# Second layer: one mask instruction for two rows on GpSimd, and the right operand packed on VectorE

## The chip, the cores and the metric

The kernel runs on one core of one Trainium2 chip. The metric is the device time of one launch in microseconds. The engines are TensorE (PE in the profile, PEld for its weight loads), VectorE (DVE), ScalarE (ACT), GpSimd (POOL) and SyncE (SP), which here only starts DMAs.

## The reference

The input `x` is a grid of 256 x 256 tokens with 64 channels. Four layers follow each other, each `x = x + layer(group_norm(x))`. The second one, on which everything here turns, is, cut to what matters:

```python
xn = layernorm(x, norm_w, norm_b)
m = mask[..., None]
left  = jnp.einsum('bijd,hd->bijh', xn, w_left)  * m
right = jnp.einsum('bijd,hd->bijh', xn, w_right) * m
left  = (left  * sigmoid(xn @ w_lgate.T)).astype(jnp.bfloat16)
right = (right * sigmoid(xn @ w_rgate.T)).astype(jnp.bfloat16)
out = jnp.einsum('bikh,bjkh->bijh', left, right).astype(jnp.float32)
out = layernorm(out, onorm_w, onorm_b) * sigmoid(xn @ w_ogate.T)
return jnp.einsum('bijh,dh->bijd', out, w_out)
```

`left` and `right` are two 256 x 256 matrices for each of the 64 channels, and the product over `k` is one matrix product for each channel. The first layer is the same in float32; the third and fourth have no mask.

## The kernel before

Each layer runs in three stages, one behind the other, with all engines joining between them.

**The projection** (`project`, for layers 1, 2 and 4) goes over the tokens in 128 steps of half the grid's rows: a step is 512 columns, two rows of the grid for each half, 64 steps in all. A step is written in parts with leads over each other, and every engine runs its own list in a fixed order:

- TensorE: `spread` (L615), `center` (L593, 16 steps ahead), `variance` (L604, 15 ahead), `heads` for both rows (L628), `out_gate` (L635 to L637). `heads` of a row waits until VectorE has read the last step's product of that row out of its bank (`pair_read`).
- ScalarE: the two passes of `square` (L672, L674, 16 steps ahead), a sigmoid for each row (L691), every eighth step `root` with its two table loads, and the output gate (L705).
- VectorE: `norm` two steps ahead (L755, L756), every eighth step the split of the inverse roots into bf16 terms (`split_high`, L731 and L733, and a step later, `split_low`, L739 and L741), then for each row the product of gate and projection (L774), which raises `pair_read`.
- GpSimd: `low_part` two steps ahead (L835), then the mask. In the second layer that is `mask_rows` (L812): it waits for both rows' products, multiplies the left half of both rows in one instruction (L824) and the right half in one for each row (L828). Each L828 raises `lr_done` by one, and the sigmoid two steps on waits for it, since it writes the slot that the mask reads.

The masked rows go into a stage of 16 rows, in one of two buffers, in bf16. Which order the elements have there differs: the left block has 16 channels, each with a run of 16 rows, `(h i)`; the right block has 16 rows, each with a run of 16 channels, `(i h)`. From the stage SP stores the blocks of all 16-channel groups but the first to DRAM, and the first group to its place in SBUF.

**The triangle product** (`triangle`, L988) takes the 64 channels in four groups of 16. The first group is in SBUF already; SP loads the others (L1031), two buffers in turn. For each channel TensorE makes four matmuls of 256 columns (L1070). Their moving operand is the left block in runs of 16 rows. Their stationary operand is, in the second layer, the right block read in place with a stride of 16 channels (`right_of`); in the other layers VectorE first copies it into consecutive columns (`pack`, L1094), into a ring of four or two. In the second layer ScalarE rounds each result to bf16 into a ring of four (L1144), and the rounded matrix is then written into `O`, where a token's channels are neighbours, by GpSimd for even channels (L1132) and by VectorE for odd ones (`spread_out`, L1106). VectorE does nothing else in this stage of this layer.

**The output** (`output`) normalizes, gates, multiplies and adds the residual. The change does not touch it.

Of the kernel before, what the change touches and what calls it, by code (L numbers as in the profile page):

```python
# [28 lines left out]
ALU = mybir.AluOpType  # L29
# [4 lines left out]
P = 128  # L34
S = 256
# [4 lines left out]
ROWS = CH // S  # L40
# [404 lines left out]
def project(nc, n, kind, low, HG, x, a, left_right, blocks, c, k, ps):  # L445
# [11 lines left out]
    with ExitStack() as ctx:  # L457
        def sb(name, shape, dt=F32):
            return ctx.enter_context(nc.sbuf_tensor(f"{name}_{n}", shape, dt))

        xs, zs, sq = sb("xs", [P, 8, CH]), sb("zs", [P, 16, CH]), sb("sq", [P, 2, CH])
        log_var, r, r_rest = sb("log_var", [P, P]), sb("r", [P, P]), sb("r_rest", [P, P])
# [3 lines left out]
        sig, gates = sb("sig", [P, 4, CH]), sb("gates", [P, 4, CH])  # L466
        paired = low == BF16
        stage0 = sb("stage0", [P, 2, 2, 2, C // HG, SEG * HG], low)
        stage = [stage0[:], last_stage(blocks, low, C // HG)]
# [325 lines left out]
        @block.gpsimd  # L795
        def _(pool):
            def mask_pair(i, q, row):
                m = i * BODY + q
                b = q // SCH
                if q % SCH == 0 and row == 0:  # L800

                    pool.wait_ge(c[f"lr_out{b}"].sem, c[f"lr_out{b}"](i * 16 * SEG_PARTS))
                    pool.wait_ge(c[f"first_out{b}"].sem, c[f"first_out{b}"](i * 64))
                pool.wait_ge(c["pair_read"].sem, c["pair_read"](m * 2 + row + 1))
                product = sig[:, (2 * q + row) % 4, :].rearrange("p (a e) -> p a e", a=4)

                by_g = k["mask"][:].rearrange("p g b i -> p (g b) i")
                mk = by_g[:, :, bass.ds(m * ROWS + row, 1)].to_broadcast([P, 4, P])
                pool.tensor_tensor(staged(b, q, row), product, mk,
                                   ALU.mult).then_inc(c["lr_done"].sem, 1)  # L810

            def mask_rows(i, q):  # L812
                m = i * BODY + q
                b = q // SCH
                if q % SCH == 0:
                    pool.wait_ge(c[f"lr_out{b}"].sem, c[f"lr_out{b}"](i * 16 * SEG_PARTS))
                    pool.wait_ge(c[f"first_out{b}"].sem, c[f"first_out{b}"](i * 64))
                pool.wait_ge(c["pair_read"].sem, c["pair_read"](m * 2 + 2))
                slot, at = 2 * q % 4, q % SCH * ROWS
                product = sig[:, slot:slot + 2, :].rearrange("p r (c l n h) -> p l c n h r", c=4, l=2, h=HG)  # L820
                by_g = k["mask"][:].rearrange("p g b i -> p (g b) i")
                mk = by_g[:, :, bass.ds(m * ROWS, ROWS)].unsqueeze(2)
                left = stage[b][:, :, :, 0].rearrange("p g b n (h i) -> p (g b) (n h) i", h=HG)[:, :, :, at:at + ROWS]
                pool.tensor_tensor(left, product[:, 0].rearrange("p c n h r -> p c (n h) r"),  # L824
                                   mk.to_broadcast([P, 4, P // 2, ROWS]), ALU.mult)
                for row in range(ROWS):
                    right = stage[b][:, :, :, 1].rearrange("p g b n (i h) -> p (g b) n i h", h=HG)[:, :, :, at + row]
                    pool.tensor_tensor(right, product[:, 1, :, :, :, row],  # L828
                                       mk[:, :, :, row:row + 1].to_broadcast([P, 4, P // 2 // HG, HG]), ALU.mult).then_inc(c["lr_done"].sem, 1)

            def low_part(i, q):
                m = i * BODY + q
                pool.wait_ge(c["xn_done"].sem, c["xn_done"](m + 1))
                pool.wait_ge(c["hi_done"].sem, c["hi_done"](m + 1))
                pool.tensor_tensor(lo[:, q % 4, :], xn[:, q % 2, :], hi[:, q % 4, :], ALU.subtract).then_inc(c["lo_done"].sem, 1)  # L835

            def step(i, q, more):
                if more(NORM):
                    low_part(i, q + NORM)
                if paired:  # L840
                    mask_rows(i, q)
                elif masked:
                    for row in range(ROWS):
                        mask_pair(i, q, row)

            for q in range(NORM):
                low_part(0, q)
            bodies_of(pool, step)
# [139 lines left out]
def triangle(nc, n, turned, low, H, HG, left_right, blocks, O, c, k, ps):  # L988
# [6 lines left out]
    rounded_first = low == BF16  # L995
    RING = 2 if turned else 4
    with ExitStack() as ctx:  # L997
        left, right = blocks[:, 0], blocks[:, 1]
        stays = turns == 1
        packed = None if rounded_first else ctx.enter_context(nc.sbuf_tensor(f"packed{n}", [P, RING, 2, S], low))  # L1000
        rounded = ctx.enter_context(nc.sbuf_tensor(f"rounded{n}", [P, 4, 2 * S], BF16)) if rounded_first else None
        right_t = ctx.enter_context(nc.sbuf_tensor(f"right_t{n}", [P, 2, 2, S], F32)) if turned else None
        block = ctx.enter_context(nc.Block())

        def channel(t, s, h):
            return t * (2 * HG) + (s * HG + h)

        def right_of(s, h):
            return right[:, s].rearrange("p b s (i h) -> p b (s i) h", h=HG)[:, :, :, h]

        def rows_of(block, s, h):

# [8 lines left out]
        def loaded(t, s):  # L1021

            return c[f"lr_in{s}"](t * 32 + 32 * s)
# [19 lines left out]
        @block.tensor  # L1043
        def _(pe):
            def turn(t, s, h):

                ch = channel(t, s, h)
                pe.wait_ge(c["packed"].sem, c["packed"](ch + 1))
                pe.wait_ge(c["tr_copied"].sem, c["tr_copied"](ch - 1))
                for kb in range(2):  # L1050
                    for jb in range(2):
                        at = kb * S + jb * P
                        last = pe.transpose(ps[2 + h % 2][:, 0, at:at + P],
                                            packed[:, h % RING, jb, kb * P:kb * P + P], k["ident"][:])
                last.then_inc(c["tr_done"].sem, 1)

            def contract(t, s, h):
                ch = channel(t, s, h)
                if turned:
                    pe.wait_ge(c["tr_copied"].sem, c["tr_copied"](ch + 1))  # L1060
                elif not rounded_first:
                    pe.wait_ge(c["packed"].sem, c["packed"](ch + 1))
                pe.wait_ge(c["o_copied"].sem, c["o_copied"](ch - 3))
                for jb in range(2):
                    for kb in range(2):
                        stationary = (right_t[:, h % 2, kb, jb * P:jb * P + P] if turned
                                      else right_of(s, h)[:, kb, jb * P:jb * P + P] if rounded_first
                                      else packed[:, h % RING, kb, jb * P:jb * P + P])
                        moving = rows_of(left, s, h)[:, kb]
                        last = pe.matmul(ps[h % 4 // 2][:, h % 2, jb * S:jb * S + S], stationary,  # L1070
                                         moving, start=(kb == 0), stop=(kb == 1))
                last.then_inc(c["tri_done"].sem, 1)

            with pe.Fori(0, turns) as t:
                for s in range(2):
                    if not stays:
                        pe.wait_ge(c[f"lr_in{s}"].sem, loaded(t, s))
                    if turned:
                        turn(t, s, 0)
                    for h in range(HG):  # L1080
                        if turned and h + 1 < HG:
                            turn(t, s, h + 1)
                        contract(t, s, h)

        @block.vector
        def _(dve):
# [17 lines left out]
            def spread_out(ch):  # L1104
                dve.wait_ge(c["o_copied"].sem, c["o_copied"](ch + 1))
                dve.tensor_copy(o_of(ch), rounded_of(ch % 4)).then_inc(c["o_stored"].sem, 1)  # L1106

            if rounded_first:
                for ch in range(1, H, 2):
                    spread_out(ch)  # L1110
            else:
                with dve.Fori(0, turns) as t:
                    for s in range(2):
                        if turned:
                            pack(t, s, 0)
                        for h in range(HG):
                            if not turned:
                                pack(t, s, h)
                            else:
                                if h + 1 < HG:  # L1120
                                    pack(t, s, h + 1)
                                turned_copy(t, s, h)
# [26 lines left out]
    if not stays:  # L1149
        c["lr_out1"].advance(16 * SEG_PARTS)  # L1150
        for s in range(2):
            c[f"lr_in{s}"].advance(32 * (turns - 1 + s))
    for name in ("tri_done", "o_copied") + (() if rounded_first else ("packed",)) + (("tr_done", "tr_copied") if turned else ()):
        c[name].advance(H)
    for name in ("o_stored", "o_moved") if rounded_first else ():
        c[name].advance(H // 2)
# [511 lines left out]
```

## Time and profile before

| what | value |
|---|---|
| median of 3 runs | 2036.54 us (2034.92 to 2039.62) |
| profiled execution, its time | 2034.19 us |
| profiled execution, its span | 2032.4 us |
| PE busy | 1688.6 us (83%) |
| ACT busy | 1370.8 us (67%) |
| DVE busy | 1291.2 us (64%) |
| POOL busy | 1027.6 us (51%) |
| second layer's projection, steady part, by the trace | 690 to 868 us |
| the same, last 16 steps | 868 to 923 us |
| second layer's triangle product | 927 to 987 us |

Times in the rows below count from the start of the span. In a timeline a row is start, duration (both us), engine, line, operation, output and input with their shapes, and the count of instructions merged into the row; in brackets stands how long the engine had been idle and what ended that. In a table of groups the two numbers behind the bar are the sum in us and the mean of one in ns. PEclk is the clock granted to TensorE as a share of full speed.

### The profile page before, as it was taken

Reading aid. Unit: us, or ns where it says so; the run is one execution under the profiler, and the core shown is the slowest. Engines: PE = TensorE matmul, PEld = TensorE weight load, DVE = VectorE, ACT = ScalarE, POOL = GpSimd, SP = SyncE. Lnnn points to the kernel's source line nnn. Section 1 sums busy time; section 2 is a strip of 40 time slices with the busy share of each in tenths; the row PEclk is TensorE's granted clock in tenths of the full one; section 3 lists DMA queues with packets and bytes.
Section 4 is the critical chain, followed back from the end, with each engine's and each line's share of the span. In section 5 each row is a group of like instructions: output and inputs, shape, how many; then the busy total and the mean of one; then the engine's idle time right before and its main releaser. Section 6 shows DMA issues by size and latency. Waiting matters only on the chain. (4 is left out here: it accounts for less than half of the span.)

```text
span 2032.4 us, 42880 instructions
## 1 busy us (share of the span) xinstructions
PE 1688.6 (83%) x11445; PEld 1000.8 (49%) x11541; DVE 1291.2 (64%) x2896; ACT 1370.8 (67%) x2541; POOL 1027.6 (51%) x1044
## 2 busy tenths in 40 slices
PE   0798986897998799975699799799779997799776
PEld 0244443785553345544355477644234444588433
DVE  7377776125763477775876388466367789344675
ACT  0598884465996799965599566477578887344555
POOL 0077777004991489896899100089222223000599
PEclk9899998998998899997799899999899999899899
DMA  8458876874997366647499665189638877754699
GB/s 335 139 171 268 253 251 211 312 292 157 368 364 246 98 199 210 196 166 275 146 367 365 213 221 203 37 320 392 213 115 247 274 250 245 264 230 183 213 401 378
DMA packets 336169, 497.39 MB, mean 245 GB/s; under 512 B 32172, under 2 KB 197679, under 8 KB 329655
## 3 DMA queue, kind: packets, MB, share of 16 engines
q1 hardware_dynamic: 336054, 496.08, 69.9%
q8 instruction: 46, 0.75, 0.2%
q14 instruction: 69, 0.56, 0.1%
HBM read 285.08 MB, written 197.13 MB: 237 GB/s over the span
## 5 line engine op out<-in xcount | busy, mean ns | idle before, releaser
L835 POOL TENSOR_TENSOR lo<-xn,hi 128x512 f16<-128x512 f32 x192 | 222.5, 1159 | 372.6 <-DVE hi L760 214.9
L628 PE MATMUL ps<-w_heads,hi 64*128 64x256 f16 x3072 | 293.7, 272 | 30.0 <-DVE sig L774 9.6
L691 ACT ACTIVATE sig<-ps,largest 128x512 f32<-128x512 f32 x384 | 253.2, 694 | 44.5 <-PE ps L628 31.5
L1146 ACT ACTIVATE O<-ps 128x512 f32 (+1 forms) x144 | 151.6, 1053 | 183.8 <-PE ps L1070 183.8
L1383 POOL TENSOR_TENSOR shared<-O,out_rs 128x128 f32<-128x128 f32 (+1 forms) x112 | 76.4, 684 | 368.9 <-DVE out_rs L1283 367.9
L774 DVE SCALAR_TENSOR_TENSOR sig<-ps,largest,sig 128x512 f32<-128x512 f32 x256 | 180.3, 745 | 119.5 <-ACT sig L691 119.0
L593 PE MATMUL ps<-xs,center 128*128 128x512 f32 x384 | 212.7, 637 | 23.7 <-DMA r_terms<-terms 16.0
L1431 PEld LDWEIGHTS ps<-ident,shared 128*128 128x128 f32 (+1 forms) x1024 | 120.5, 133 | 225.3 <-issue 96.5
L1431 PE MATMUL ps<-ident,shared 128*128 128x128 f32 (+1 forms) x1024 | 160.7, 282 | 76.6 <-POOL shared L1383 50.0
L628 PE MATMUL ps<-w_heads,lo 64*128 64x256 f16 x1536 | 212.7, 271 | 0.0
L672 ACT ACTIVATE zs<-ps,shift 128x512 f32<-128x512 f32 x192 | 132.6, 690 | 107.7 <-PE ps L593 102.3
L628 PEld LDWEIGHTS ps<-w_heads,hi 64*128 64x128 f16 x3072 | 153.9, 94 | 101.2 <-issue 47.0
L1272 DVE BATCH_NORM_STATS2 out_bn<-O 128x6 f32 (+2 forms) x1024 | 194.4, 256 | 12.5 <-PEq L997 12.3
L1369 POOL TENSOR_TENSOR shared<-O,out_bn 128x512 f32<-128x512 f32 x128 | 134.7, 1053 | 133.4 <-DVE out_bn L1272 133.4
L1394 POOL TENSOR_TENSOR shared<-shared 128x512 f32<-128x512 f32 x128 | 162.7, 1278 | 14.9 <-DMA x_dram<-shared 6.3
L1070 PE MATMUL ps<-shared,right_t 128*128 128x256 f32 x640 | 154.3, 387 | 3.6 <-DVE right_t L1101 3.4
L705 ACT ACTIVATE gates<-ps,largest 128x512 f32<-128x512 f32 x192 | 133.4, 695 | 32.8 <-DMA gate<-gates 27.7
L1292 DVE TENSOR_TENSOR shared<-ps,shared 128x512 f32<-128x512 f32 x128 | 88.5, 691 | 95.6 <-ACT ps L1469 92.7
L1448 PE MATMUL ps<-shared,w_out 128*128 128x512 f32 x256 | 139.0, 627 | 7.7 <-ACT shared L1473 5.8
L1383 POOL TENSOR_TENSOR shared<-shared,out_rs 128x512 f32<-128x512 f32 x128 | 133.3, 1042 | 20.2 <-DVE out_rs L1283 20.2
L756 DVE TENSOR_TENSOR xn<-zs,ps 128x512 f32<-128x512 f32 x192 | 130.2, 678 | 12.8 <-remote 11.2
L1442 PE MATMUL ps<-shared,w_out 128*128 128x512 f32 x256 | 132.8, 601 | 0.0
(167 smaller groups left out, 3556.4 us busy)
## 6 DMA issues: line engine op xcount, KB each, us to landing
shared<-left_right SPq DMA_DIRECT2D x34, 2048.0 KB, 12.0
shared<-gate SPq DMA_DIRECT2D x224, 256.0 KB, 4.6
gate<-gates SPq DMA_DIRECT2D x96, 512.0 KB, 3.9
x_dram<-shared SPq DMA_DIRECT2D x192, 256.0 KB, 4.3
shared<-x_dram SPq DMA_DIRECT2D x192, 256.0 KB, 4.6
xs<-x_dram SPq DMA_DIRECT2D x64, 512.0 KB, 4.3
left_right<-stage SPq DMA_DIRECT2D x64, 448.0 KB, 4.9
left_right<-shared SPq DMA_DIRECT2D x64, 448.0 KB, 4.4
```

The lines of the kernel that those rows point to most:

```text
L593: pe.matmul(bank, k["center"][:], xs[:, q % 8, :], start=True, stop=True).then_inc(c["z_done"].sem, 1)
L628: last = pe.matmul(PAIR[row][:, g, kb * S:kb * S + S], tokens[half, q % 4, at:at + P], k["w_heads"][half, part, :], start=(step == 0), sto ...
L691: act.activation(sig[:, slot, :].rearrange("p (c e) -> p c e", c=4), pair(row, 0), ACT.Sigmoid, scale=k["largest"][:, 0:1]).then_inc(c["si ...
L774: dve.scalar_tensor_tensor(dst, pair(row, 1), k["largest"][:, 1:2], factor, ALU.mult, ALU.mult).then_inc(pair_read.sem, 1)
L835: pool.tensor_tensor(lo[:, q % 4, :], xn[:, q % 2, :], hi[:, q % 4, :], ALU.subtract).then_inc(c["lo_done"].sem, 1)
L1070: last = pe.matmul(ps[h % 4 // 2][:, h % 2, jb * S:jb * S + S], stationary, moving, start=(kb == 0), stop=(kb == 1))
L1146: act.activation(o_of(ch), ps[h % 4 // 2][:, h % 2, :].rearrange("p (b g i) -> p b g i", b=2, g=2), ACT.Copy).then_inc(c["o_copied"].sem, 1)
L1272: last = dve.bn_stats(bn[:, b, jb, at:at + 2, :].rearrange("p g s -> p (g s)"), tokens.rearrange("p g h -> p h g"))
L1383: pool.tensor_tensor(scaled[:, q % RING], tokens, per_token(rs[:].unsqueeze(4), q), ALU.mult).then_inc(c["scaled"].sem, 1)
L1394: pool.tensor_tensor(xo[:, q % RING, :], og[:, q % RING], xs[:, q % RING, :], ALU.add).then_inc(c["x_new"].sem, 1)
L1431: last = pe.transpose(TURNED[q % 4][:, at:at + P], scaled[:, q % RING, jb, 2 * row:2 * row + 2, :].rearrange("p g h -> p (g h)"), k["ident ...
L1448: mm = pe.matmul(OUT[q % 4], k["w_out"][:], u[:, q % RING], start=True, stop=True)
```

## The change

In the projection of the second layer the right block of a stage gets the order of the left one, 16 channels with a run of 16 rows each. The three mask instructions of a step become one, which takes both rows and both halves, 1024 columns, and raises `lr_done` by two at its end.

In the triangle product the right operand of the second layer is no longer read in place. VectorE copies it channel by channel into the ring `packed` of four, as the other layers do, and TensorE waits for the copy. VectorE's list becomes: pack an even channel, pack the odd one behind it, then write out the odd channel of the pair before. A pack waits until the matmuls of four channels earlier are done, and the first of a group also for the group's load.

```diff
-                product = sig[:, slot:slot + 2, :].rearrange("p r (c l n h) -> p l c n h r", c=4, l=2, h=HG)
+                product = sig[:, slot:slot + 2, :].rearrange("p r (c e) -> p c e r", c=4)
                 by_g = k["mask"][:].rearrange("p g b i -> p (g b) i")
-                mk = by_g[:, :, bass.ds(m * ROWS, ROWS)].unsqueeze(2)
-                left = stage[b][:, :, :, 0].rearrange("p g b n (h i) -> p (g b) (n h) i", h=HG)[:, :, :, at:at + ROWS]
-                pool.tensor_tensor(left, product[:, 0].rearrange("p c n h r -> p c (n h) r"),
-                                   mk.to_broadcast([P, 4, P // 2, ROWS]), ALU.mult)
-                for row in range(ROWS):
-                    right = stage[b][:, :, :, 1].rearrange("p g b n (i h) -> p (g b) n i h", h=HG)[:, :, :, at + row]
-                    pool.tensor_tensor(right, product[:, 1, :, :, :, row],
-                                       mk[:, :, :, row:row + 1].to_broadcast([P, 4, P // 2 // HG, HG]), ALU.mult).then_inc(c["lr_done"].sem, 1)
+                mk = by_g[:, :, bass.ds(m * ROWS, ROWS)].unsqueeze(2).to_broadcast([P, 4, P, ROWS])
+                rows = stage[b].rearrange("p g b l n (h i) -> p (g b) (l n h) i", h=HG)[:, :, :, at:at + ROWS]
+                pool.tensor_tensor(rows, product, mk, ALU.mult).then_inc(c["lr_done"].sem, 2)
...
-        packed = None if rounded_first else ctx.enter_context(nc.sbuf_tensor(f"packed{n}", [P, RING, 2, S], low))
+        packed = ctx.enter_context(nc.sbuf_tensor(f"packed{n}", [P, RING, 2, S], low))
...
-                elif not rounded_first:
+                else:
                     pe.wait_ge(c["packed"].sem, c["packed"](ch + 1))
...
                         stationary = (right_t[:, h % 2, kb, jb * P:jb * P + P] if turned
-                                      else right_of(s, h)[:, kb, jb * P:jb * P + P] if rounded_first
                                       else packed[:, h % RING, kb, jb * P:jb * P + P])
...
             if rounded_first:
-                for ch in range(1, H, 2):
-                    spread_out(ch)
+                for ch in range(H):
+                    pack(ch // (2 * HG), ch // HG % 2, ch % HG)
+                    if ch >= 2 and ch % 2 == 1:
+                        spread_out(ch - 2)
+                spread_out(H - 1)
```

## Rows read from the trace of the kernel before

**Rows 1.** The page's first part: busy time, share and instructions of each engine.

```profile
PE 1688.6 (83%) x11445; PEld 1000.8 (49%) x11541; DVE 1291.2 (64%) x2896; ACT 1370.8 (67%) x2541; POOL 1027.6 (51%) x1044
```

**Rows 2.** Busy time by stretch: length, then PE, PEld, DVE, ACT, POOL, PEclk, DMA.

```profile
690.00:868.00 178.00, 169.42 (x1765) 89.74 (x1786) 132.15 (x211) 162.10 (x258) 157.37 (x186) 1.00 0.59 191
868.00:923.00 55.00, 37.68 (x422) 22.71 (x423) 40.24 (x63) 33.61 (x52) 53.10 (x65) 0.96 0.48 164
946.50:987.00 40.50, 30.98 (x192) 22.15 (x192) 35.89 (x24) 28.32 (x48) 35.80 (x24) 0.88 0.48 195
```

**Rows 3.** Timeline of PE, second layer's projection: L635, one in each step.

```profile
786.57 0.39 PE L635 MATMUL ps<-hi,w_gate 128*128 128x512 f16 x1
...
790.16 0.39 PE L635 MATMUL ps<-hi,w_gate 128*128 128x512 f16 x1
...
793.76 0.39 PE L635 MATMUL ps<-hi,w_gate 128*128 128x512 f16 x1
```

**Rows 4.** Timeline of POOL, second layer's projection.

```profile
785.87 1.12 POOL L824 TENSOR_TENSOR shared<-sig,mask 128x512 bf16<-128x512 f32 x1 [3.02 <-DVE sig L774]
...
875.22 1.11 POOL L824 TENSOR_TENSOR stage<-sig,mask 128x512 bf16<-128x512 f32 x1 [1.09 <-DVE sig L774]
...
878.96 1.12 POOL L824 TENSOR_TENSOR stage<-sig,mask 128x512 bf16<-128x512 f32 x1 [0.28 <-DVE sig L774]
...
882.31 1.11 POOL L824 TENSOR_TENSOR stage<-sig,mask 128x512 bf16<-128x512 f32 x1
...
884.54 1.16 POOL L835 TENSOR_TENSOR lo<-xn,hi 128x512 f16<-128x512 f32 x1
...
921.27 1.19 POOL L828 TENSOR_TENSOR shared<-sig,mask 128x256 bf16<-128x256 f32 x2
```

**Rows 5.** Groups by line and shape, POOL, second layer's projection.

```profile
L828 POOL TENSOR_TENSOR shared<-sig,mask 128x256 bf16<-128x256 f32 x64 | 38.5, 622 | 0.0
...
L824 POOL TENSOR_TENSOR shared<-sig,mask 128x512 bf16<-128x512 f32 x32 | 35.6, 1113 | 10.4 <-DVE sig L774 10.1
```

**Rows 6.** Timeline of DVE, second layer's projection, at a split.

```profile
786.81 0.27 DVE L739 CAST terms<-r_rest 128x128 bf16<-128x128 f32 x1
787.11 0.61 DVE L741 TENSOR_TENSOR terms<-r_rest,terms 128x128 bf16<-128x128 f32 x1
787.64 1.40 DVE L774 SCALAR_TENSOR_TENSOR sig<-ps,largest,sig 128x512 f32<-128x512 f32 x2
```

**Rows 7.** Timeline of POOL, DVE and PE, first layer's projection, at a split.

```profile
141.38 1.08 POOL L809 TENSOR_TENSOR shared<-sig,mask 128x512 f32<-128x512 f32 x1
...
141.73 0.39 PE L635 MATMUL ps<-hi,w_gate 128*128 128x512 f16 x1
...
142.58 1.12 DVE L741 TENSOR_TENSOR terms<-r_rest,terms 128x128 bf16<-128x128 f32 x1
...
143.62 1.40 DVE L774 SCALAR_TENSOR_TENSOR sig<-ps,largest,sig 128x512 f32<-128x512 f32 x2
...
145.84 0.39 PE L635 MATMUL ps<-hi,w_gate 128*128 128x512 f16 x1
```

**Rows 8.** Waits in the triangle product: engine, line, releaser, us, times, longest.

```profile
PE ps L1070 <- DMA shared<-left_right: 8.9, 1, 8.9
```

**Rows 9.** Timeline of the triangle product behind that load.

```profile
946.78 5.54 PE L1070 MATMUL ps<-shared 128*128 128x256 bf16 x25 [8.94 <-DMA shared<-left_right]
...
948.72 1.15 POOL L1132 CAST O<-rounded 128x512 bf16 x1 [6.85 <-ACT rounded L1144]
...
949.36 1.10 DVE L1106 CAST O<-rounded 128x512 f32<-128x512 bf16 x1 [6.94 <-ACT rounded L1144]
```

**Rows 10.** Timeline of POOL, the rest of the triangle product.

```profile
953.83 32.43 POOL L1132 CAST O<-rounded 128x512 bf16 x21 [0.62 <-ACT rounded L1144]
```

**Rows 11.** Groups by line and shape, DVE, whole span: copies from SBUF to SBUF.

```profile
L1094 DVE COPY packed<-shared 128x512 f32<-128x512 f32 x144 | 58.1, 421 | 115.6 <-PE ps L1070 50.2 <-DMA shared<-left_right 49.9 <-PEq L457 11.5
...
L388 DVE CAST w_heads<-w_both 128x256 f16<-128x256 f32 x3 | 0.9, 294 | 0.1
```

More of the change, by code:

```diff
@@ L1006, in channel @@
             return t * (2 * HG) + (s * HG + h)
-        def right_of(s, h):
-            return right[:, s].rearrange("p b s (i h) -> p b (s i) h", h=HG)[:, :, :, h]
         def rows_of(block, s, h):
@@ L1152, in triangle @@
             c[f"lr_in{s}"].advance(32 * (turns - 1 + s))
-    for name in ("tri_done", "o_copied") + (() if rounded_first else ("packed",)) + (("tr_done", "tr_copied") if turned else ()):
+    for name in ("packed", "tri_done", "o_copied") + (("tr_done", "tr_copied") if turned else ()):
         c[name].advance(H)
```

## The prediction

> **What bounds the kernel now.** The engine totals come first [rows 1]: no engine is busy for the whole span, so each stage has to be read by itself. The change touches two stages, both in the second of the four layers: its projection (690 to 923 us) and its triangle product (927 to 987 us). Beside them stands the table of busy time by stretch [rows 2].
>
> In the first part of the projection (690 to 868) all engines but VectorE are over 88% busy, so busy shares don't name the bound; the distance between equal instructions does. TensorE's first output-gate matmul (L635) comes every 3.60 us, at 786.57, 790.16, 793.76 [rows 3], whether GpSimd had idled or was behind. GpSimd needs less: where it runs without a gap, one step's masks start 882.31 - 878.96 = 3.35 us behind the last step's, of which 884.54 - 882.31 = 2.23 are the three mask instructions and 1.12 the low part [rows 4]. So TensorE paces this part, and every eighth step ScalarE's table loads add to it. The reader is to see that time taken from GpSimd is worth nothing here.
>
> The last 16 steps have no centering and no squares left, TensorE gets light, and GpSimd is busy 53.10 of 55 us [rows 2]. From the mask at 878.96 to the end at 922.5 it runs without a gap: 14 masks, the last of whose parts starts at 921.27 [rows 4]. Here GpSimd is the bound.
>
> In the triangle, TensorE waits 8.9 us once, for the load of the second group of channels [rows 8]; the first 16 channels end before it, so what they lose, up to that, is free. The other 48 channels go from 946.78 to 987 [rows 2, 9] in pairs: GpSimd writes out one channel of a pair (L1132), VectorE the other (L1106). 21 of GpSimd's take 32.43 us, about 1.67 each while both run, so one starts every (32.43 - 1.67) / 20 = 1.54, say 1.55 us [rows 10]. Alone, one takes 1.15. At the start of the group GpSimd's ends at 948.72 + 1.15 = 949.87 and VectorE's, begun at 949.36, ends at 950.46 [rows 9]: 0.59 us behind the other's end, though it lay beside it for 0.51. The two exclude each other. A pair is VectorE's 0.59 and GpSimd's remaining 0.96, and 1.55 is their sum.
>
> **The change, part by part.**
>
> *The mask instruction.* One of 512 columns takes 1.113 us, one of 256 takes 0.622 [rows 5]: 1.92 ns a column. 1024 columns in one instruction take 1.113 + 512 x 0.00192 = 2.10 us, and start to start 2.06, as neighbours overlap by 0.04. Three instructions took 2.23. Saving 0.17 a step; bounds 0 (twice 1.113) and 0.35 (if the second half cost one 0.622 and the fixed part 0.18 vanished too). For 48 steps that is hidden behind TensorE and worth 0; in the 14 masks of the end it is 14 x 0.17 = -2.4 us.
>
> The left operand's mask already read its two rows innermost, rows 2 KB apart, as the new one does. The Trainium skill (GPSIMD Engine Reference, section 7, Performance pitfalls for Q7 kernels) says that GpSimd pays about 2.9 cycles an element instead of 1.9 where its innermost read step is over 8 bytes. By that the new instruction would take an estimated 1024 x 2.9 / 1.2 GHz = 2.47 us and the end would lose about 3 us instead of gaining 2.4, and the sum below would be 2059. The trace does not agree: 512 columns with the wide step cost 1.113, less than two of 256 with the narrow step (1.244).
>
> *Row 0 comes free later.* Its slot was free after the left and the first right part, 1.113 + 0.622 less overlap or some 1.7 us into the mask, now after 2.10. The sigmoid two steps on needs it. Between the end of one mask and the start of the next but one lie 1.12 + 2.06 + 1.12 = 4.3 us, and in it go one row's sigmoid and both products (1.40 [rows 6]), about half of it. Cost 0; with that cover gone, 0.4 a step.
>
> *VectorE behind a longer GpSimd instruction.* There are eight batches of eight steps, and in the loop VectorE seven times splits the inverse roots in small instructions (L731 to L741). In this layer L739 starts at 786.81 inside the left mask (785.87 to 786.99), ends 0.08 after it, L741 ends 0.15 behind the next part, and L774 starts at 787.64 [rows 4, 6]. In the first layer, whose mask parts take 1.08, the same L741 ran into the low part and took 1.12 instead of 0.61; L774 starts 1.16 us behind the mask's end (142.46 to 143.62), and 143.62 - 141.73 = 1.89 behind that step's L635 instead of 787.64 - 786.57 = 1.07. TensorE's next step came 4.11 us later, not 3.60 [rows 3, 6, 7]. So of 0.82 of delay 0.31 is slack and 0.51 is paid. Now the mask covers 785.87 to 787.97, L739 waits to its end, the low part gets in front of L741, and L774 starts at 787.97 + 1.16 = 789.13: 1.49 later, of which 1.18 is paid. The split's terms leave SP one step later in its order, so no transfer is late. TensorE is then at its 3.60 again and makes nothing up. Six of the seven places cost 1.18. At the seventh the mask from 875.22 would end at 877.32, both products at 877.32 + 1.16 + 1.40, and the mask of 878.96 start at 879.97: 1.0, in front of the GpSimd-bound end. Sum 6 x 1.18 + 1.0 = +8.1; bounds 0 (the small instructions get in first) and 7 x 1.5 = 10.5. Projection: 8.1 - 2.4 = +5.7 us.
>
> *The packs.* 64 copies of 512 bf16 columns join VectorE, and two stand ahead of each of its write-outs. The trace has no bf16 copy. The same copy in f32 takes 0.421; 256 columns of f32 (the same bytes) take 0.294 [rows 11]. Both lie on 0.167 + 0.5 ns a column. I take 0.29, by the bytes, and keep 0.42 for the range. If they were to run beside GpSimd freely, VectorE's pair would need 2 x 0.29 + 0.59 + 0.17 = 1.34, under 1.55: cost 0. But what excludes the write-out excludes the pack: GpSimd 0.96, one pack whose start hides behind it 0.29 - 0.16 = 0.13, the other 0.29, the write-out with its start 0.75: 2.13 instead of 1.55, +0.58. 24 pairs: +13.9. The first three were paced by TensorE at 25 matmuls in 5.54 us, some 1.7 a pair, so -0.4; the first matmul waits for one pack, +0.3. Triangle: +13.8. Bounds: with every start hidden +0.26 a pair, 6 us; with packs of 0.42, 2.39 a pair, +20.
>
> That a copy on VectorE waits out a running GpSimd instruction is also what the Trainium skill says (SBUF — State Buffer, Who interferes with whom): whoever issues first has the shared port pair for the whole instruction. The trace agrees for casts and two-input operations (L741's 1.12 above); for a bf16 copy no row shows it, and the page raises the chance of the forecast over the rival without exclusion.
>
> *TensorE's weights* come from consecutive columns instead of a stride; it is not the bound in the pairs: 0. *The loads* of later groups are issued when channels 16 and 32 are done, later by what the pairs lose, and the pairs use them later by as much: 0.
>
> **Sum.** The profiled run took 2034.2 us (span 2032.4). 2034.2 + 5.7 + 13.8 = 2053.7. The runs shown have their median at 2036.5, 2.3 above it. I predict 2054.
>
> **The rivals.**
> - *The ports are shared, not excluded* (not slower): packs lie beside GpSimd's write-outs, splits beside the mask; what stays is -2.4, 2032. It decides if pairs stay at 1.55. For it: no row shows a bf16 copy beside GpSimd. Against it: the 0.59 behind the other's end [rows 9] and L741's 1.12 [rows 7]. 8%.
> - *GpSimd paces the whole projection*: 64 x 0.17 = -10.9, the packs +13.8: 2037. For it: 157 of 178 us busy. Against: steps 3.60 apart while it needs 3.35 [rows 3, 4]. 6%.
> - *Only the packs cost*: the small splits get in before the mask: 13.8 - 2.4, 2046. 16%.
> - *Packs of 0.42, or waits twice a pair*: 5.7 + 20, 2060. 14%.
> - *Only the splits cost*: starts and packs hide in the triangle's waits: 2040. 6%.
>
> **How the numbers follow.** The forecast has 50%, with its own range 2047 to 2060. The range 2038 to 2067 leaves out the first two rivals and little above. About 0.2%, 4 us, is what a measurement tells from no change. Faster by more holds half of the first rival and a little of the second, 6%; within 0.2% 9%; slower 85%.
>
> **What would show it.** Right: a mask instruction near 2.10 us; L739 over 1 us and L741 near 1.1 at six places, TensorE's step behind them 4.8 instead of 3.60; GpSimd's masks at the end 3.18 apart; packs near 0.29 when alone, longer beside L1132; pairs 2.1 apart, the stretch from the second load to the last write-out 54 us instead of 40. Wrong: pairs at 1.55, or steps of 3.60 throughout, or projection steps shorter than 3.60 before its end.

## The result, and the profile after

The changed kernel took 2052.98 us (median of 4 runs, 2048.48 to 2053.8), the kernel before, run beside it, 2038.08: ratio 1.0061, 95% interval 1.0044 to 1.0078, or 9 to 16 us slower. Timed again later it took 2048.91 (6 runs) against 2038.85, ratio 1.0061 again (1.0045 to 1.0078). These ratios are estimates over the runs; the medians alone give 1.0073 and 1.0049, that is 15 and 10 us. The forecast was 2054, slower. The three profiled runs of the changed kernel have spans of 2050.8, 2043.7 and 2047.8 us.

To read a span of 2050 us for a loss of 12, cut it at three marks: TensorE's second L635 in the second layer's projection, the end of the last mask, the first `BATCH_NORM_STATS2` of the output stage. Up to the first mark (690.81 us before, 689.70, 691.02 and 692.48 in the three profiles after) and behind the last (1045.3 before, 1048.4, 1045.7, 1048.3 after) lies code that the change doesn't touch: it scatters by 3 us here, and in some runs below the part behind the last mark takes up to 1052.6. So the stages between the marks tell more than the whole time:

| us | first L635 mark to last mask | last mask to output stage |
|---|---|---|
| before | 231.65 | 64.68 |
| after, first profile | 237.46 (+5.8) | 75.29 (+10.6) |
| after, second | 236.80 (+5.2) | 70.21 (+5.5) |
| after, third | 236.83 (+5.2) | 70.23 (+5.5) |

The projection, which has 64 steps of 512 columns (64 L635, not 128), loses 5.2 to 5.8 in each. The triangle loses 5.5 in two and 10.6 in one: the same program has two rhythms there.

The engine totals and the same kind of stretches as [rows 1, 2], first profile:

```profile
PE 1692.1 (83%) x11445; PEld 997.9 (49%) x11541; DVE 1314.1 (64%) x2960; ACT 1370.2 (67%) x2541; POOL 1003.3 (49%) x916
```

```profile
690.00:868.00 178.00, 163.47 (x1689) 85.75 (x1710) 140.37 (x203) 157.36 (x249) 140.44 (x90) 1.00 0.60 191
868.00:927.50 59.50, 43.37 (x487) 26.93 (x493) 47.75 (x70) 38.18 (x59) 54.02 (x35) 0.96 0.45 152
951.00:1002.50 51.50, 31.34 (x192) 19.44 (x192) 41.09 (x74) 26.97 (x49) 28.65 (x24) 0.84 0.38 156
```

GpSimd is 24 us less busy in the whole and the kernel is slower. In the steady part of the projection TensorE went from 169.42 to 163.47 of 178 us: something makes it wait.

What does is seen at a split, which answers to [rows 3, 4, 6]. PE, POOL and DVE of the first profile:

```profile
788.92 0.39 PE L635 MATMUL ps<-hi,w_gate 128*128 128x512 f16 x1
...
793.67 0.39 PE L635 MATMUL ps<-hi,w_gate 128*128 128x512 f16 x1
```

```profile
788.23 2.04 POOL L824 TENSOR_TENSOR shared<-sig,mask 128x1024 bf16<-128x1024 f32 x1 [3.31 <-DVE sig L774]
790.22 1.16 POOL L830 TENSOR_TENSOR lo<-xn,hi 128x512 f16<-128x512 f32 x1
```

```profile
789.16 1.19 DVE L739 CAST terms<-r_rest 128x128 bf16<-128x128 f32 x1
790.38 1.15 DVE L741 TENSOR_TENSOR terms<-r_rest,terms 128x128 bf16<-128x128 f32 x1
791.45 1.40 DVE L774 SCALAR_TENSOR_TENSOR sig<-ps,largest,sig 128x512 f32<-128x512 f32 x2
```

L739 ends at 790.35, 0.08 behind the mask (790.27); L741 at 791.53, 0.15 behind the low part (791.38). In the kernel before they took 0.27 and 0.61 there [rows 6], and 0.61 was part wait already: at the start of the second layer of the kernel before, where GpSimd does nothing yet, L741 takes 0.29:

```profile
663.95 0.29 DVE L741 TENSOR_TENSOR terms<-r_rest,terms 128x128 bf16<-128x128 f32 x1
```

L774 now starts 791.45 - 788.92 = 2.53 behind L635 instead of 1.07 [rows 3, 6], and TensorE's step is 793.67 - 788.92 = 4.75 instead of 3.60; six steps of the projection are. The high split of the same batch, a step earlier, waits longer too (L731 0.98 and L733 1.14, before 0.64 and 0.61), but the step behind it stays at 3.98 as before: there the delay is hidden.

The end, where GpSimd is the bound, on POOL, and the group by shape (L830 is the low part, L1126 the write-out):

```profile
876.30 2.03 POOL L824 TENSOR_TENSOR stage<-sig,mask 128x1024 bf16<-128x1024 f32 x1
...
881.11 2.04 POOL L824 TENSOR_TENSOR stage<-sig,mask 128x1024 bf16<-128x1024 f32 x1 [1.68 <-DVE sig L774]
...
885.87 2.04 POOL L824 TENSOR_TENSOR stage<-sig,mask 128x1024 bf16<-128x1024 f32 x1 [1.61 <-DVE sig L774]
...
889.61 2.04 POOL L824 TENSOR_TENSOR stage<-sig,mask 128x1024 bf16<-128x1024 f32 x1 [0.59 <-DVE sig L774]
...
892.73 2.04 POOL L824 TENSOR_TENSOR stage<-sig,mask 128x1024 bf16<-128x1024 f32 x1
```

```profile
L824 POOL TENSOR_TENSOR stage<-sig,mask 128x1024 bf16<-128x1024 f32 x32 | 65.3, 2040 | 26.8 <-DVE sig L774 26.8
...
L1126 POOL CAST O<-rounded 128x512 bf16 x32 | 37.9, 1199 | 36.5 <-ACT rounded L1138 36.5
```

One mask instruction takes 2.04 us; without a gap the masks are 3.11 to 3.12 apart instead of 3.35 [rows 4]. From 889.61 on there are ten such distances, and two more without a low part between.

The triangle's copies on VectorE, groups of the first profile, and what the engines waited for there (engine, line, releaser, us, times, longest):

```profile
L1085 DVE COPY packed<-shared 128x512 bf16<-128x512 bf16 x64 | 31.2, 528 | 11.3 <-PEq L457 7.0 <-DMA shared<-left_right 4.3
L1097 DVE CAST O<-rounded 128x512 f32<-128x512 bf16 x32 | 29.3, 916 | 12.4 <-ACT rounded L1138 12.4
```

```profile
PE ps L1061 <- DVE packed L1085: 34.2, 27, 8.8
...
DVE O L1097 <- ACT rounded L1138: 12.4, 14, 2.1
...
DVE packed L1085 <- DMA shared<-left_right: 4.3, 1, 4.3
```

TensorE now waits for VectorE's packs, where before its one long wait was for the load [rows 8]. The shortest pack takes 0.267 us, the median 0.311.

The two rhythms, on DVE: first profile, then second profile with its POOL:

```profile
966.12 1.29 DVE L1097 CAST O<-rounded 128x512 f32<-128x512 bf16 x1 [0.74 <-ACT rounded L1138]
967.23 1.41 DVE L1085 COPY packed<-shared 128x512 bf16<-128x512 bf16 x2
968.56 0.73 DVE L1097 CAST O<-rounded 128x512 f32<-128x512 bf16 x1
969.10 0.51 DVE L1085 COPY packed<-shared 128x512 bf16<-128x512 bf16 x2
970.43 1.30 DVE L1097 CAST O<-rounded 128x512 f32<-128x512 bf16 x1 [0.82 <-ACT rounded L1138]
```

```profile
973.45 0.73 DVE L1097 CAST O<-rounded 128x512 f32<-128x512 bf16 x1
973.98 1.37 DVE L1085 COPY packed<-shared 128x512 bf16<-128x512 bf16 x2
975.26 0.72 DVE L1097 CAST O<-rounded 128x512 f32<-128x512 bf16 x1
975.80 1.36 DVE L1085 COPY packed<-shared 128x512 bf16<-128x512 bf16 x2
```

```profile
974.02 1.18 POOL L1126 CAST O<-rounded 128x512 bf16 x1 [0.64 <-ACT rounded L1138]
```

In the second VectorE never idles and a pair takes 975.26 - 973.45 = 1.81; its two packs end at 975.35, 0.15 behind GpSimd's instruction (975.20). In the first the distances alternate, 968.56 - 966.12 = 2.44 and 1.87, so two pairs take 4.31. The first of the two meets two write-outs of GpSimd in a row, and its write-out takes 1.29 and its packs 1.41; the second meets none and takes 0.73 and 0.51, and then VectorE idles 0.7 to 0.8 for a rounded channel that isn't there yet. The other engines keep the same rhythm. PE and POOL of the first profile, then PE of the second:

```profile
968.58 2.01 PE L1061 MATMUL ps<-shared,packed 128*128 128x256 bf16 x16 [2.29 <-DVE packed L1085]
970.07 2.58 POOL L1126 CAST O<-rounded 128x512 bf16 x2 [1.77 <-ACT rounded L1138]
```

```profile
974.35 0.61 PE L1061 MATMUL ps<-shared,packed 128*128 128x256 bf16 x4 [0.16 <-DVE packed L1085]
```

With the alternation TensorE makes four channels in one go and then waits 2.3 us, GpSimd two and then waits 1.8; without it each goes channel by channel.

### The profile page after: what moved, and what is told of

The parts are those of the page before. It is cut to its first block and busy times, and to the rows that moved or that the text cites. A ratio compares the mean times of both kernels' runs of the same rounds, so it can differ in the third digit from the quotient of the medians.

```text
span 2050.8 us, 42850 instructions
## 1 busy us (share of the span) xinstructions
PE 1692.1 (83%) x11445; PEld 997.9 (49%) x11541; DVE 1314.1 (64%) x2960; ACT 1370.2 (67%) x2541; POOL 1003.3 (49%) x916
## 5 line engine op out<-in xcount | busy, mean ns | idle before, releaser
L830 POOL TENSOR_TENSOR lo<-xn,hi 128x512 f16<-128x512 f32 x192 | 222.3, 1158 | 375.6 <-DVE hi L760 218.7
L774 DVE SCALAR_TENSOR_TENSOR sig<-ps,largest,sig 128x512 f32<-128x512 f32 x256 | 180.2, 745 | 108.4 <-ACT sig L691 108.2
L1061 PE MATMUL ps<-shared,packed 128*128 128x256 f32 (+1 forms) x768 | 158.6, 367 | 50.8 <-DVE packed L1085 50.1
L1085 DVE COPY packed<-shared 128x512 f32<-128x512 f32 (+1 forms) x208 | 89.3, 454 | 126.7 <-DMA shared<-left_right 52.7
L1061 PEld LDWEIGHTS ps<-shared,packed 128*128 128x128 f32 (+1 forms) x768 | 126.5, 169 | 83.2 <-DVE packed L1085 42.3
L705 ACT ACTIVATE gates<-ps,largest 128x512 f32<-128x512 f32 x192 | 133.4, 695 | 32.0 <-DMA gate<-gates 27.1
L1442 PE MATMUL ps<-shared,w_out 128*128 128x512 f32 x256 | 139.6, 630 | 8.8 <-ACT shared L1467 7.7
```

What stands on the lines that cost most here:

```text
L774: dve.scalar_tensor_tensor(dst, pair(row, 1), k["largest"][:, 1:2], factor, ALU.mult, ALU.mult).then_inc(pair_read.sem, 1)
L1442: mm = pe.matmul(OUT[q % 4], k["w_out"][:], u[:, q % RING], start=True, stop=True)
```

## The experiments

**One mask instruction, no packs.** The kernel before with only the new mask; TensorE goes on reading the right operand in place with the old stride, without regard to its new order.

```diff
-                pool.tensor_tensor(left, product[:, 0].rearrange("p c n h r -> p c (n h) r"),
-                                   mk.to_broadcast([P, 4, P // 2, ROWS]), ALU.mult)
-                for row in range(ROWS):
...
+                pool.tensor_tensor(rows, product, mk, ALU.mult).then_inc(c["lr_done"].sem, 2)
```

> The one mask instruction and the new order of the right block, but no packs: TensorE reads its stationary operand in place with the old stride, so the right operand's elements are the wrong ones and only the time counts. If the projection's loss is VectorE's small splits waiting behind a 2.04 us mask, and the triangle's loss is the packs: L739 near 1.2 us and L741 near 1.15 in the second layer, a step of 4.75 us behind each split, the last mask ends some 4.7 us later than before (922.5), the pairs of write-outs are back at 1.55 us and the stretch behind the second load at 40 us: 4.7 us slower than before in all. Rival, that the layout or the mask instruction by itself costs in the triangle too, or that packs are cheap: about 15 us slower, pairs over 1.8.

2042.79 against 2038.77: ratio 1.0026 (1.001 to 1.0042). Projection 236.85 (+5.2), triangle 64.42 (-0.3). The whole loss of the projection comes with the new mask instruction, its length or its order of elements, and the triangle's with the packs.

**Packs only, first try.** The changed kernel, but the right half's mask in one instruction for each row, as before.

```diff
-                pool.tensor_tensor(rows, product, mk, ALU.mult).then_inc(c["lr_done"].sem, 2)
+                pool.tensor_tensor(rows[:, :, 0:C], product[:, :, 0:C], mk, ALU.mult)
+                for row in range(ROWS):
+                    pool.tensor_tensor(rows[:, :, C:P, row], product[:, :, C:P, row], mk[:, :, :, row], ALU.mult).then_inc(c["lr_done"].sem, 1)
```

> The new order and the packs, but the mask again in three instructions (left 512 columns, right 256 for each row). If the length of a GpSimd instruction is what VectorE's splits wait for: L739 near 0.27 and L741 near 0.61 again, steps of 3.98 and then 3.60, the last mask ends at 922 to 923 as before, and the triangle keeps its loss, 50 to 51 us behind the second load instead of 40.4: 10.5 us slower than before in all. Rival, that writing the right block with the wide stride is what slows the projection: it stays some 5 us later, 15 in all.

A miss: 2083.56 against 2038.77, ratio 1.0217 (1.0185 to 1.025). The group of the right half on POOL, and at a split DVE and POOL:

```profile
L826 POOL TENSOR_TENSOR shared<-sig,mask 128x256 bf16<-128x256 f32 x64 | 77.6, 1416 | 0.0
```

```profile
790.23 6.55 DVE L731 CAST terms<-r 128x128 bf16<-128x128 f32 x1 [0.15 <-ACT r L684]
```

```profile
791.26 1.19 POOL L832 TENSOR_TENSOR lo<-xn,hi 128x512 f16<-128x512 f32 x1
792.42 1.10 POOL L824 TENSOR_TENSOR shared<-sig,mask 128x512 bf16<-128x512 f32 x1
793.49 2.38 POOL L826 TENSOR_TENSOR shared<-sig,mask 128x256 bf16<-128x256 f32 x2
795.49 1.20 POOL L832 TENSOR_TENSOR lo<-xn,hi 128x512 f16<-128x512 f32 x1
```

In the new layout one row's right half is single 2-byte elements 32 bytes apart, and 256 columns of them take 1.41 us instead of 0.62 [rows 5]. GpSimd becomes the bound of the projection, and a cast on VectorE waits 6.55 us through all its back-to-back instructions, to 796.78, 0.09 behind the last; at five other places it takes 2.2 to 2.4. The time says nothing on the packs' share. But the triangle, which has the changed kernel's code, says something on the rhythm: behind the load its write-outs on VectorE alternate at first (2.48, 1.78, 2.45, 1.86 apart), later they are 1.81 to 1.91 apart, eight times in a row, and it takes 73.6 us. So one run can go over from the alternation to 1.81.

**Packs only, second try.** Both rows together, but left and right half apart: two instructions of 512 columns.

```diff
-                pool.tensor_tensor(rows, product, mk, ALU.mult).then_inc(c["lr_done"].sem, 2)
+                pool.tensor_tensor(rows[:, :, 0:C], product[:, :, 0:C], mk, ALU.mult)
+                pool.tensor_tensor(rows[:, :, C:P], product[:, :, C:P], mk, ALU.mult).then_inc(c["lr_done"].sem, 2)
```

> The changed kernel's layout and packs, but the mask of a step in two instructions of 512 columns (left half of both rows, right half of both rows) instead of one of 1024, so that VectorE's splits meet instructions as long as those of the kernel before. Theory (the projection's loss comes from the length of the mask instruction, the triangle's from the packs): steps behind the splits 3.6 to 3.75, last mask ends at 921 to 923, triangle as in the changed kernel (50.9 instead of 40.4 us from the second load): +10.5 us over the kernel before, 2049. Rival A (the order of the elements, not the instruction's length, makes GpSimd and with it the projection slower): last mask ends at 926 or later, 2053. Rival B (the packs cost little, and run-to-run scatter made the rest): under 2043.

2045.29 against 2040.34: ratio 1.0021 (1.0009 to 1.0034). L635 at a split:

```profile
790.10 0.39 PE L635 MATMUL ps<-hi,w_gate 128*128 128x512 f16 x1
...
793.89 0.39 PE L635 MATMUL ps<-hi,w_gate 128*128 128x512 f16 x1
```

Step 3.79; projection 231.89 (+0.2), with the new layout and the same number of columns: length of the instruction is what costs, rival A falls. The triangle lost 5.5, not the 10.5 expected, with the changed kernel's code there: the first hint of the second rhythm.

**The low split on GpSimd.** The changed kernel, but in the second layer L739 and L741 are GpSimd's, between its low part and its mask.

```diff
+            def split_low(i, b):
...
+                pool.tensor_tensor(terms[:, 1, :], r_rest[:], zero[:].to_broadcast([P, P]), ALU.add).then_inc(parts.sem, 1)
+                pool.wait_ge(parts.sem, parts(batch * R_PARTS + 2))
+                pool.tensor_tensor(terms[:, 2, :], r_rest[:], terms[:, 1, :], ALU.subtract).then_inc(c["r_split"].sem, 1)
```

> The changed kernel with the second layer's low split (the work of L739 and L741) moved to GpSimd, in its own order between the low part and the mask, so that VectorE has nothing left there that GpSimd could hold up. Theory of exclusion: no step of 4.75 behind the splits, 3.60 instead; the projection keeps only its gain at the end, so the last mask ends 2 to 4 us earlier than before; with the packs' 10.5 some 7 us slower than before. Rival, that the longer mask delays TensorE by itself, by freeing row 0's slot later: steps of 4.75 remain and the kernel stays 15 us slower.

2042.24 against 2038.77: ratio 1.0028 (1.0013 to 1.0042). POOL at a split:

```profile
787.37 1.16 POOL L843 TENSOR_TENSOR lo<-xn,hi 128x512 f16<-128x512 f32 x1
788.49 0.40 POOL L835 TENSOR_TENSOR terms<-r_rest,zero 128x128 bf16<-128x128 f32 x1
788.97 0.43 POOL L837 TENSOR_TENSOR terms<-r_rest,terms 128x128 bf16<-128x128 f32 x1
```

All steps behind a low split are 3.60 and the projection is 229.1 us, 2.6 less than before: the masks of the end now save their 0.23. The loss was VectorE's wait behind the mask. The triangle is 69.9 us, +5.2 over before, at 1.81 a pair.

**No write-outs on GpSimd.** The changed kernel, but ScalarE writes the even channels into `O` itself, in f32 and without rounding them to bf16; GpSimd idles in the triangle.

```diff
-                        if rounded_first:
+                        if rounded_first and h % 2:
```

> The changed kernel, but in the triangle of the second layer ScalarE writes the even channels into O itself, in f32 and without the rounding to bf16, and GpSimd does nothing there. Theory of exclusion: with GpSimd gone two packs take 0.5 us and a write-out 0.72 to 0.75 always, none is stretched to 1 us or more; VectorE needs 1.25 to 1.3 a pair, so ScalarE with 0.6 + 1.05 = 1.65 sets the pair, the stretch behind the second load is some 41 us instead of 51, and the kernel is 5 to 6 us slower than before (the projection's part). Rival, that the packs cost by lying in the chain pack, matmul, copy, write-out, whatever GpSimd does: pairs stay over 2.0 us and the kernel 15 us slower.

2045.37 against 2038.77: ratio 1.0041 (1.0025 to 1.0057). VectorE's group, up to 975 us:

```profile
L1085 DVE COPY packed<-shared 128x512 bf16<-128x512 bf16 x46 | 12.3, 312 | 12.6 <-PEq L457 7.0 <-DMA shared<-left_right 5.6
```

None of the 64 packs is longer than 0.41, where 17 to 26 of 64 were over 0.5: it is GpSimd that they wait for. The triangle is 67.4 us, +2.7 over before, although the wait is gone: the pairs behind the load start 1.69 apart on average. That is near the 1.65 expected if ScalarE sets the pair, and from 956 to 990 us ScalarE is busy 31.18 of 34 us, but it still idles now and then for TensorE, so that it alone is the bound is not shown.

**Write-outs one pair later.**

```diff
-                    if ch >= 2 and ch % 2 == 1:
-                        spread_out(ch - 2)
+                    if ch >= 4 and ch % 2 == 1:
+                        spread_out(ch - 4)
+                spread_out(H - 3)
```

> The changed kernel with one edit: VectorE writes out the odd channel of two pairs before instead of one pair before, so its write-out is due a pair later. Theory (VectorE's order closes a loop: its write-out waits for ScalarE's copy, that for TensorE, that for VectorE's pack): with the write-out later VectorE never waits, all pairs run at the 1.82 us that the lower bound with every start hidden gives, and 24 pairs x (2.13 - 1.82) = 7 us or a little less go: the stretch from the second load to the output stage 50.9 -> 44 to 46, the time 2047 to 2048. Rival (the exclusion between VectorE and GpSimd alone makes 2.13 a pair, whatever the order): stretch 50 to 51, time 2053. The projection as in the changed kernel: last mask ends near 927, steps of 4.75 behind the splits.

2052.31 against 2040.34: ratio 1.0054 (1.0037 to 1.0071). Triangle 70.4 us, most pairs at 1.81. But the time is not the 2047 to 2048 expected and not below the changed kernel's, which is as it must be if that often runs at 1.81 too; in this profile the untouched part behind the triangle also takes 1052.6 us instead of 1045.3. Whether the order keeps the alternation away stays open.

**The changed kernel again, twice.** No edit.

> The changed kernel itself, timed once more and profiled once more, because two kernels with its triangle code (with the low split on GpSimd, and with the mask in two instructions) ran their pairs at 1.82 us where its first profile shows an alternation of 2.45 and 1.78. Theory A (two rhythms of one program; which one comes depends on how the first pairs behind the load fall): its stretch from the second load to the output stage may come out near 46 this time, and the time over the kernel before lies between 5.8 + 5.5 = 11 and 5.8 + 10.5 = 16 us. Theory B (the alternation belongs to this kernel, the other two differ by something in the projection): the stretch is 50 to 51 again and the difference 15 to 16.

> The changed kernel, a third profile, for the same question: theory A lets the stretch be 46 or 51, theory B wants 50 to 51. In either the projection loses the same as in the first profile: six steps of 4.75 behind the splits, masks at the end 3.11 apart.

The first took 2048.91, the second, a single run, 2049.55. Both ran at 1.81 (table and rows above): theory A. What decides between the rhythms, with the same code and the same load in front, was not found.

**The splits of the first and fourth layer on GpSimd.** The kernel before; the first layer's low split, the fourth's both, in its loop.

```diff
-                for split, lead in zip((split_high, split_low), SPLIT):
+                for split, lead in on_dve:
...
+                for split, lead in on_pool:
+                    if more(lead) and (q + lead) % BATCH == 0:
+                        split(i, (q + lead) // BATCH)
```

> The kernel before, the second layer untouched; in the loop of the first layer's projection the low split (two instructions of 128 columns), in the fourth layer's both splits run on GpSimd, between its own instructions, instead of VectorE. Theory (VectorE's small instructions wait behind GpSimd's long ones, wherever they meet; the change only brought this to the second layer): steps behind a split fall from 4.11 to 3.60 in the first layer (7 x 0.51 = 3.6 us), from 4.54 and 4.28 to 3.98 and 3.60 in the fourth (7 x 1.24 = 8.7): 12 us, 2026 to 2027. Rival (those steps are longer for another reason, the transfers of the split terms or ScalarE's table loads): 2037 to 2039. Second rival: GpSimd, busy 3.3 of 3.6 us a step in the first layer, becomes late by the 0.83 us of the split: 1st layer gains nothing, 2030.

> The kernel with the splits of the first and fourth layer on GpSimd, timed once more beside the kernel before. Its first profile shows every step behind a split at 3.60, but the first layer not shorter for it (the time came back at steps that wait for transfers), the fourth some 2 us shorter; its median was 7.5 us under that of the kernel before. Theory (what the profile shows: the saved steps are mostly given back): 2 to 4 us faster, ratio 0.998 to 0.999. Rival (the profile of before was a lucky one, and the gain is that of the medians): 7 us, ratio 0.9965.

First 2032.8 against 2040.34, ratio 0.9964 (0.9943 to 0.9984), or 3 to 12 us faster; again 2034.92 against 2038.85, ratio 0.9988 (0.9975 to 1.0000), or 0 to 5. Taken together a few us faster, and the expected 12 did not come. The first layer's L635 here:

```profile
141.49 0.39 PE L635 MATMUL ps<-hi,w_gate 128*128 128x512 f16 x1
...
145.09 0.39 PE L635 MATMUL ps<-hi,w_gate 128*128 128x512 f16 x1
...
152.29 0.39 PE L635 MATMUL ps<-hi,w_gate 128*128 128x512 f16 x1
...
158.16 0.39 PE L635 MATMUL ps<-hi,w_gate 128*128 128x512 f16 x1
```

```profile
PE ps L615 <- DMA r_terms<-terms: 2.1, 1, 2.1
```

and of the kernel before:

```profile
153.04 0.39 PE L635 MATMUL ps<-hi,w_gate 128*128 128x512 f16 x1
...
158.24 0.39 PE L635 MATMUL ps<-hi,w_gate 128*128 128x512 f16 x1
```

The step behind the split is 3.60 instead of 4.11, and the time comes back three steps on, where 5.87 stands for 5.20: there TensorE waits 2.1 us for the transfer of the split terms, 1.4 before. In the fourth layer the steps of 4.54 stay, so the high split was not their cause; those of 4.27 to 4.36 go, and from its first to its last output gate on ScalarE (L705) it takes 236.3 and 236.1 us instead of 238.6. In the first profile of the changed kernel, whose fourth layer is that of the kernel before, it takes 240.1.

**The change, mended.** The changed kernel with the low split on GpSimd in layers 1 and 2 and both in layer 4, one pack for two channels, write-outs a pair later.

```diff
+                both = right[:, s].rearrange("p b s (h i) -> p h (b s) i", h=HG)[:, h:h + 2]
+                dve.tensor_copy(packed[:, h % RING:h % RING + 2].rearrange("p h b (s i) -> p h (b s) i", i=SEG),
+                                both).then_inc(c["packed"].sem, 2)
```

> The changed kernel with its two costs mended: the low split on GpSimd in the first and second layer, both splits in the fourth; in the triangle one pack for two channels (1024 columns) and VectorE's write-out one pair later. Theory: second layer's projection ends 2.9 us before that of the kernel before; a pair costs GpSimd's 0.96, a pack of about 0.55 whose start of 0.16 is hidden, and a write-out of 0.59 to 0.75: 1.7 to 1.8 instead of 1.55, +4 to +6 us; the first and fourth layer give 12: 2038 - 3 + 5 - 12 = 2028. Rival (pairs stay at 2.13, since what GpSimd and VectorE exclude does not depend on how the packs are cut): 2037. Rival (one layer's theory is wrong and 12 us don't come): 2040.

2038.04 against 2040.34, ratio 0.9994 (0.9984 to 1.0003): no slower than before, no faster, where 2028 was expected. The second layer does what was expected, and what is missing is most of the 12 us of the first and fourth layer, as in the run above. Projection 229.1 (-2.6), triangle 68.2 (+3.5); a pair on DVE takes 1.73 (963.62 - 961.89) to 1.83:

```profile
960.06 0.43 DVE L1126 COPY packed<-shared 128x1024 bf16<-128x1024 bf16 x1
960.41 1.66 DVE L1138 CAST O<-rounded 128x512 f32<-128x512 bf16 x1
961.89 0.43 DVE L1126 COPY packed<-shared 128x1024 bf16<-128x1024 bf16 x1
...
963.62 0.43 DVE L1126 COPY packed<-shared 128x1024 bf16<-128x1024 bf16 x1
```

## Why the prediction was right, point by point

- *The mask instruction*: 2.10 forecast, 2.04 measured, and 0.23 a step saved instead of 0.17. By the rule that was weighed there (the Trainium skill, GPSIMD Engine Reference, section 7, Performance pitfalls for Q7 kernels) it would have been an estimated 2.47; the trace does not bear that out. In the 48 steps that TensorE paces the saving is worth nothing, as forecast: with the splits out of the way they stayed at 3.60. At the end it is worth 2.6, forecast 2.4. The bounds put the fixed part of an instruction at 0.18; the means of [rows 5] give 0.622 - 256 x 0.00192 = 0.13, which the sum does not use.
- *VectorE behind the mask*: L739 1.19 and L741 1.15 at six places, steps of 4.75 (forecast 4.8): L774 comes 1.46 later and 1.15 of it is paid, so the slack is the forecast 0.31. Six times 1.15 is 6.9; the seventh place costs 1.0, as worked out (distance of 885.87 - 881.11 = 4.76 instead of 3.74), and in the first profile the one behind it 0.4 (3.74 instead of 3.35). There 13 instead of 14 masks run without a gap, since the late start shifts the bound; they take 37.55 us instead of 40.15, -2.6. Sum 5.7; measured 5.8 in this profile, 5.2 in the others, where the distance behind the seventh place is 3.11, and forecast 5.7. The one-mask run, the mask in two instructions and the low split on GpSimd show cause and cure. The Trainium skill says the same of L741 (SBUF — State Buffer, Who interferes with whom): a two-input VectorE instruction contends with a GpSimd instruction that reads SBUF, and the shared ports are an exclusive lock; the trace agrees with 1.15 for 0.29 alone.
- *The packs*: 0.27 to 0.31 (forecast 0.29), and they do wait for GpSimd: rivals with shared ports fall. The first 16 channels' loss lies under the load, as forecast (VectorE's 4.3 us of wait for it).
- *The pair* is the term that was mis-sized. 2.13 was built from one start hidden and one paid, and 13.8 us from it. In two profiles of three a pair takes 1.81, which is the lower bound that the prediction gave (every start hidden, 1.55 + 0.26), and the triangle loses 5.5. In the one with the alternation two pairs take 4.31, 2.16 each, and all pairs behind the load 2.05 on average, close to 2.13, but not for the reason given: the engines go by four channels, and once in two pairs VectorE waits 0.7 to 0.8 for ScalarE, which the prediction did not have. It loses 10.6.
- *The sum*: 5.2 + 5.5 = 10.7 us in two profiles, 16.4 in the first, and 9 to 16 by the runs, against 19.5 forecast: the direction was right, and so were both causes, but the pair made the size too large. That 2054 lies 1 us from the first median is in part luck. The sum started from a profiled run of 2034.2, while the kernel before, timed beside the changed one, took 2038.08; from there the same sum gives 2057.6. And the first median was on the high side; the second, 2048.91, is 4 us lower.
- *The rival "only the packs cost"* (2046) is near the second median by number, but its mechanism fell: the splits do not get in first. *Packs of 0.42* fell with 0.31, *GpSimd paces the whole projection* with the steps that stay at 3.60, *only the splits cost* with the 5.5 us and more of the triangle.

## What to carry to other kernels

Merging instructions on GpSimd makes each one that VectorE's small instructions wait behind longer; count VectorE's casts, copies and two-input operations that meet it before counting the saved overhead (here some 8 us paid for 2.6 saved). Time that is taken from an engine that does not pace its stage is worth nothing, and time saved at one step can come back at the next wait for a transfer. Where two engines exclude each other, bound a new copy by its work without its start as well as with it, and read more than one profile before believing a rhythm.

## What the runs showed of the hardware

- GpSimd's cost went by how it writes: 1024 columns with two neighbouring bf16 elements at a time took 2.04 us (2.0 ns each), 256 columns of single elements 32 bytes apart 1.41 (5.5 ns), 256 in runs 0.62. The 256 columns were read in the same order in both.
- A VectorE cast that waited for GpSimd was not always next in turn: one was passed over by a row of back-to-back instructions for 6.55 us.
- The same triangle code on the same data ran at 1.81 us a pair or at an alternating 2.44 and 1.87, 5 us apart in one stage, and one run went over from the second to the first.
